# Two heads of attention on one core: TensorE in groups of two slots, 32-column tiles for all sums, denominators inverted through transposes, the subtraction shared out anew

## The chip, the cores and the metric

The kernel runs on one NeuronCore of a Trainium2 chip. The metric is the time of one execution on the device in microseconds (us), the median of the runs of a kernel. Engines are named as in the profile: PE is TensorE (matmuls; PEld its weight loads), DVE is VectorE, ACT is ScalarE, POOL is GpSimd, SP is SyncE, which issues most DMAs.

## The reference, cut to what matters

Two layers of self-attention over 2304 positions (48 x 48), with 2 images, 512 channels, 8 heads of 64. Layer 0 has a group norm in front; layer 1 adds a position embedding to what q and k are made of. All is float32.

```
# layer 0: x is (2, 512, 48, 48)
xn  = group_norm(x)
qkv = qkv_w @ xn + qkv_b            # per head: q, k, v of (64, 2304)
w   = softmax((q.T @ k) * 64**-0.5) # (2304, 2304) for each of 16 heads
x   = proj_w @ (v @ w.T) + proj_b + x
# layer 1: the same with other weights; q and k from [x, embedding], then
x   = softmax(q.T @ k / 8) @ v @ Wout + bout + x
```

## The kernel before, in words

Five stages follow one another: norm, q/k/v projection, attention of layer 0, projection out and q/k/v of layer 1, attention of layer 1, projection out. The change touches the attention stage alone (`attention_stage`), which runs twice.

A block is 384 queries of one pair of heads (e = 0, 1). There are 48 blocks in a stage, 96 in all. The 2304 keys are 18 tiles (kt) of 128, in 6 chunks (c) of 3. A block has 12 slots, s = 2c + e: one chunk of keys with one head. The work of a block is spread over some 30 slots, and each engine runs, slot by slot, a fixed list written out in its own `body`. At slot s of block t:

- TensorE (lines 735 to 748) waits until the banks of scores are free (`bank_free`: the copy of slot s - 2 is done, since slots use two sets of three PSUM banks in turn), makes the scores of slot s (L700: six matmuls of 128x128 by 384 columns), and then the sums of the slot 18 earlier (`weigh`): probabilities by v (L713, "PV", in 64-column tiles, one per head, bank 6) and probabilities by ones (L721, the denominators, in 32-column tiles, bank 7). Each float32 matmul of the sums is two records in the profile. `PV_TILES` and `DEN_PAIRS` say how many tiles of keys each slot takes: 1 or 2 (3 once, none once) and 0 to 2 pairs.
- VectorE takes the running maximum over keys (L851, from slot 2 of a block), at slots 10 and 11 also folds three running maxima into one (L856, L858), and subtracts the maximum from its part of the columns of the slot 15 earlier (`shift`, helper at L618: query columns 0 to 128 of 384, of three tiles).
- GpSimd subtracts the other columns (also L618: 128 to 384). It waits for the copy of the scores and, for the first two slots of a block, for the maximum; it runs as far ahead as these let it.
- ScalarE takes the exponential of the slot 16 earlier (L769), in place, which waits for both subtractions of it, and then copies the scores of slot s from PSUM into `prob` (L756) after VectorE's maximum has read them (from slot 2).

The maximum over the partitions goes through TensorE: `turn` at slots 0 and 1 (L677, transposes of the folded maxima), `reduce` on VectorE (L837), `broadcast_max` at slots 2 and 3 (L683, transposes), `copy_max` on ScalarE (L763). Slots 4 and 5 of TensorE also wait for that copy. The denominators: ScalarE copies the sums out (L781), TensorE spreads them by a matmul with a matrix of ones and zeros (L689, slot 8), ScalarE copies (L787), VectorE inverts in six parts of 64 columns (L871), and `norm` multiplies (L878). Waits on semaphores carry all of this order; SP loads q, k and v by the progress of `scored` and `pv_done`.

Of the kernel before, what the change touches and what calls it, by code (L numbers as in the profile page):

```python
# [7 lines left out]
ALU = mybir.AluOpType  # L8
# [3 lines left out]
P = 128  # L12
# [18 lines left out]
SHIFT_DVE = 128  # L31
# [3 lines left out]
PV_TILES = [[0, 1], [2], [3, 4], [5], [6, 7], [8], [9, 10], [11], [12, 13], [14], [15, 16, 17], []]  # L35
DEN_PAIRS = [[], [0], [], [1, 2], [], [3], [], [4, 5], [], [6], [], [7, 8]]
PV_END = 10
FREE_AT = [3, 3, 7, 7, 11, 11]
REDUCE_AT, BROADCAST_AT, SPREAD_AT = 0, 2, 8
INVERT_AT = [9, 12, 12, 13, 13, 14]  # L40
PARTS = len(INVERT_AT)
NORM_AT, STORE_AT = 3, 4
# [495 lines left out]
def attention_stage(nc, name, psum, bufs, qk_d, v_d, att_d, next_loads):  # L538
# [4 lines left out]

    with ExitStack() as ctx:  # L544
# [5 lines left out]
        den, dsp, pvr, rec, ob = bufs["den"], bufs["dsp"], bufs["pvr"], bufs["rec"], bufs["ob"]  # L550
        ones, sel, ident = bufs["ones"], bufs["sel"], bufs["ident"]
# [25 lines left out]
        def pv_count(t, v):  # L577
            return 2 * SLOTS + SLOTS * t + v + 1
# [51 lines left out]
        def _(sp):  # L630
            with sp.Fori(0, B) as b, sp.Fori(0, PAIRS) as hp:
                pair = b * PAIRS + hp
                for j in range(JB):
# [28 lines left out]
        def _(pe):  # L662
            pe.sem_inc(scored, 2 * SLOTS)
            pe.sem_inc(pv_done, 2 * SLOTS)

            def bank_free(t, s):
# [4 lines left out]
                if not before(t, 2) and s == SPREAD_AT + 2 and live(t - 2):  # L671
                    pe.wait_ge(spread_copied, t - 1)
# [32 lines left out]
            def weigh(t, par, v):  # L705
                if v == 0 and not before(t, 1):
                    pe.wait_ge(pv_copied, t)
                for kt in PV_TILES[v]:
                    if kt % 3 == 0:
                        pe.wait_ge(v_in[kt // 3], 16 * (t // JB + 1))  # L710
                        pe.wait_ge(exp_done, SLOTS * t + 2 * (kt // 3) + 2)
# [14 lines left out]
            def body(t, par):  # L726
                for s in range(SLOTS):
                    bank_free(t, s)
                    if not before(t, 1) and live(t - 1):
                        if s in (REDUCE_AT, REDUCE_AT + 1):  # L730
                            turn(t - 1, s, s - REDUCE_AT)
                        if s in (BROADCAST_AT, BROADCAST_AT + 1):
                            broadcast_max(t - 1, s, s - BROADCAST_AT)
                    if not before(t, 2) and live(t - 2) and s == SPREAD_AT:
                        spread_den(t - 2, s)
                    if live(t):
                        scores(t, par, s)
                    tv, pv, v = behind(t, par, s, PV_LAG)
                    if live(tv):
                        weigh(tv, pv, v)  # L740
# [4 lines left out]
        def _(act):  # L745
# [25 lines left out]
            def copy_weighted(t, par):  # L771
                act.wait_ge(pv_done, pv_count(t, PV_END))
                if not before(t, 2):
                    act.wait_ge(normed, t - 1)
                nc.scalar.activation(pvr[par][:, :], pv_bank, ACT.Copy).then_inc(pv_copied, 1)

            def copy_den(t):
                act.wait_ge(pv_done, pv_count(t, SLOTS - 1))
                if not before(t, 1):
                    act.wait_ge(spread, t)  # L780
                nc.scalar.activation(den[:, :], den_bank, ACT.Copy).then_inc(den_copied, 1)  # L781

            def copy_spread(t, s):
                act.wait_ge(spread, t + 1)
                if not before(t, 1):
                    act.wait_ge(inverted, PARTS * t)
                nc.scalar.activation(three(dsp[:, :]), spare(s), ACT.Copy).then_inc(spread_copied, 1)  # L787
# [8 lines left out]
            def body(t, par):  # L796
                for s in range(SLOTS):
                    te, pe_, se = behind(t, par, s, EXP_LAG)
                    if live(te):
                        exponential(te, pe_, se)  # L800
                    if s == 5 and not before(t, 2) and live(t - 2):
                        copy_weighted(t - 2, par)
                    if s == 6 and not before(t, 2) and live(t - 2):
                        copy_den(t - 2)
# [4 lines left out]
                    if s == SPREAD_AT and not before(t, 2) and live(t - 2):  # L809
                        copy_spread(t - 2, s)  # L810
# [8 lines left out]
        def _(pool):  # L819
            with pool.Fori(0, NB // 2) as it:  # L820
                for par in range(2):
                    t = 2 * it + par
                    for s in range(SLOTS):
                        if s < 2:
                            pool.wait_ge(mx_ready, unit(t, s))
                        pool.wait_ge(copied, SLOTS * t + s + 1)
                        shift_part(nc.gpsimd, par, s, SHIFT_DVE, CH).then_inc(pool_shifted, 1)

        @block.vector
        def _(dve):  # L830
# [35 lines left out]
            def invert(t, part):  # L866
                dve.wait_ge(spread_copied, t + 1)
# [5 lines left out]
            def norm(t, par):  # L873
                dve.wait_ge(inverted, PARTS * (t + 1))
# [3 lines left out]
                nc.vector.tensor_tensor(ob[par][:, :], pvr[par][:, :], rec[:, :], ALU.mult).then_inc(normed, 1)  # L878

            def body(t, par):  # L880
                for s in range(SLOTS):
                    if s in (REDUCE_AT, REDUCE_AT + 1) and not before(t, 1) and live(t - 1):
                        reduce(t - 1, s, s - REDUCE_AT)
# [5 lines left out]
                    for part in range(PARTS):  # L889
                        if INVERT_AT[part] == s and not before(t, 2) and live(t - 2):  # L890
                            invert(t - 2, part)
                        if INVERT_AT[part] == s + SLOTS and not before(t, 3) and live(t - 3):
                            invert(t - 3, part)
                    if s == NORM_AT and not before(t, 3) and live(t - 3):
                        norm(t - 3, 1 - par)
# [4 lines left out]
def program(nc, x, params, qkv_w, qkv_bv, proj_w, w1, w1v, w1e, wout, emb, consts, out):  # L900
# [9 lines left out]
    with ExitStack() as ctx:  # L910
        const_sb = sb_(ctx, nc, "const_sb", [P, 32 + 3 * P])
        par_sb = sb_(ctx, nc, "par_sb", [P, 2 * CT + 2 * CT + CT + CT])
        ones, sel, gmat = const_sb[:, 0:32], const_sb[:, 32:32 + P], const_sb[:, 32 + P:32 + 2 * P]
        ident = const_sb[:, 32 + 2 * P:32 + 3 * P]
# [157 lines left out]
```

## Time and profile before

| | |
|---|---|
| median of 3 runs | 4704.73 us (4703.88 to 4705.93) |
| the profiled execution | 4705.96 us, span of its instructions 4703.8 us |
| busy share of the span | PE 97%, PEld 52%, DVE 71%, ACT 60%, POOL 49% |
| granted TensorE clock, mean | 0.993 |
| attention stages | from about 410 to 2225 us and 2750 to 4570 us |

The profile is read in this order: the busy shares, the groups by line (how often, how long, what the idle time before them waited for), and then the timeline of each engine in one block. Ends of matmuls are modelled, so the distance from one start to the next says more about TensorE than the durations. "<-" names what ended an idle time.

### The profile page before, as it was taken

To read this page: it belongs to the slowest core of one execution; us is meant where nothing else is said; L and a number is where in the kernel's file an instruction comes from. 1 tells how busy PE (TensorE), PEld (TensorE's weight loads), DVE (VectorE), ACT (ScalarE), POOL (GpSimd) and SP (SyncE) were. 2 spreads that over 40 slices of the span, in tenths; PEclk is the share of its full clock that TensorE was granted. 3 is DMA by queue.
4 is the path that set the end of the run, shared out by engine and by line. 5 is a ranking of instruction groups with operands and counts; after the bars stand their busy time and mean duration, and the time that the engine had idled before them with its cause. 6 is when DMAs were issued, how large, how long until landed. Compare 5 with 4: busy or idle time off the path is not lost. (4 is left out here: it accounts for less than half of the span.)

```text
span 4703.8 us, 77022 instructions
## 1 busy us (share of the span) xinstructions
PE 4551.0 (97%) x25368; PEld 2453.8 (52%) x25368; DVE 3318.6 (71%) x3948; ACT 2820.0 (60%) x2981; POOL 2314.1 (49%) x1160
## 2 busy tenths in 40 slices
PE   7997999999999999998999979999999999999989
PEld 4554555555555555554555545555555555555545
DVE  4224888888888888888433358888888888888872
ACT  1113777777777777776001137777777777777750
POOL 0001666666666666666100026666666666666650
PEclk9999999999999999999999999999999999999999
DMA  4334121211111111110444431111111111111206
GB/s 192 131 124 118 25 61 28 54 35 45 42 45 45 37 45 35 48 43 32 167 146 149 147 104 31 50 38 42 46 41 45 37 47 34 50 37 45 59 20 214
DMA packets 234728, 321.66 MB, mean 68 GB/s; under 512 B 12080, under 2 KB 221104, under 8 KB 233648
## 3 DMA queue, kind: packets, MB, share of 16 engines
q1 hardware_dynamic: 214512, 292.61, 21.3%
q10 hardware_dynamic: 20160, 28.32, 1.6%
q8 instruction: 34, 0.56, 0.0%
q14 instruction: 22, 0.18, 0.0%
HBM read 188.76 MB, written 132.12 MB: 68 GB/s over the span
## 5 line engine op out<-in xcount | busy, mean ns | idle before, releaser
L618 POOL TENSOR_TENSOR prob<-prob,mx 128x768 f32<-128x768 f32 x1152 | 2293.1, 2025 | 2227.6 <-ACT mx L763 2227.6
L756 ACT ACTIVATE prob<-psum_att 128x1152 f32<-128x1152 f32 x1152 | 1302.3, 1130 | 587.1 <-DVE run L851 510.5
L700 PE MATMUL psum_att<-qst,kst 128*128 128x384 f32 x6912 | 1513.4, 354 | 44.6 <-DMA kst<-qk_scratch 27.4
L769 ACT ACTIVATE prob<-prob 128x1152 f32<-128x1152 f32 x1152 | 1340.8, 1164 | 356.2 <-DVE prob L618 355.2
L700 PEld LDWEIGHTS psum_att<-qst,kst 128*128 128x128 f32 x6912 | 1156.5, 189 | 452.3 <-issue 427.1
L713 PE MATMUL psum_att<-prob,vst 128*64 128x384 f32 x6912 | 1348.3, 502 | 15.4 <-ACT prob L769 9.2
L851 DVE TENSOR_TENSOR run<-psum_att,run 128x1152 f32<-128x1152 f32 x768 | 1039.1, 1353 | 370.1 <-PE psum_att L700 359.8
L618 DVE TENSOR_TENSOR prob<-prob,mx 128x384 f32<-128x384 f32 x1152 | 1015.5, 882 | 1.7 <-ACT mx L763 1.7
L713 PEld LDWEIGHTS psum_att<-prob,vst 128*64 128x64 f32 x6912 | 405.4, 136 | 532.1 <-issue 491.0
L721 PE MATMUL psum_att<-prob,const_sb 128*32 128x384 f32 x6912 | 677.1, 494 | 0.0
L321 PE MATMUL psum<-xc_l,wq 128*128 128x384 f32 x1536 | 504.1, 489 | 10.8 <-DVE hl_l L426 5.6
L851 DVE TENSOR_TENSOR run<-psum_att,prob 128x1152 f32<-128x1152 f32 x192 | 260.5, 1357 | 269.4 <-PE psum_att L700 269.3
L321 PEld LDWEIGHTS psum<-xc_l,wq 128*128 128x128 f32 x1536 | 293.8, 191 | 221.7 <-issue 20.3
L721 PEld LDWEIGHTS psum_att<-prob,const_sb 128*32 128x32 f32 x6912 | 165.6, 108 | 424.9 <-issue 423.7
L364 ACT ACTIVATE hl_l<-qk_sum 128x384 fp32r<-128x384 f32 x96 | 50.1, 522 | 444.9 <-DVE qk_sum L423 444.9
L871 DVE RECIPROCAL rec<-dsp 128x64 f32<-128x64 f32 x576 | 287.0, 526 | 12.1 <-ACT dsp L787 12.1
L186 PE MATMUL psum<-attc_l,wo_l 128*128 128x384 f32 x768 | 252.6, 490 | 6.3 <-PEq L544 6.3
L858 DVE TENSOR_TENSOR fold<-fold,run 128x384 f32<-128x384 f32 x192 | 248.7, 1295 | 6.6
L367 ACT ACTIVATE hl_l<-psum,par_sb 128x384 fp32r<-128x384 f32 x96 | 55.8, 581 | 309.2 <-PE psum L321 309.2
L186 PEld LDWEIGHTS psum<-attc_l,wo_l 128*128 128x128 f32 x768 | 147.2, 192 | 109.1 <-issue 8.9
L430 DVE SCALAR_TENSOR_TENSOR hl_l<-psum,par_sb,hl_l 128x384 fp32r<-128x384 f32 x96 | 59.3, 618 | 188.6 <-ACT hl_l L367 188.6
L677 PEld LDWEIGHTS psum_att<-const_sb,fold 128*128 128x128 f32 x576 | 59.9, 141 | 161.7 <-DVE fold L858 139.6
(53 smaller groups left out, 1633.6 us busy)
## 6 DMA issues: line engine op xcount, KB each, us to landing
qk_scratch<-hl_l SPq DMA_DIRECT2D x48, 1536.0 KB, 5.6
qst<-qk_scratch SPq DMA_DIRECT2D x192, 384.0 KB, 5.4
kst<-qk_scratch SPq DMA_DIRECT2D x192, 192.0 KB, 3.3
v_scratch<-vo_l SPq DMA_DIRECT2D x24, 768.0 KB, 3.5
vst<-v_scratch SPq DMA_DIRECT2D x96, 192.0 KB, 2.5
att_scratch<-ob ACTq DMA_DIRECT2D x96, 192.0 KB, 1.9
attc_l<-att_scratch SPq DMA_DIRECT2D x24, 768.0 KB, 6.0
x_sb<-in_x SPq DMA_DIRECT2D x8, 1152.0 KB, 14.3
```

Source lines behind the costliest of these rows:

```text
L186: mm = nc.tensor.matmul(bank, w[c], att[:, c, :], start=(c == 0), stop=(c == CT - 1))
L321: mm = nc.tensor.matmul(qk_bank(m), qkv["w"][:, c, m * P:(m + 1) * P], xc[p][:, c, :], start=(c == 0), stop=(c == CT - 1))
L618: return engine.tensor_tensor(x[:, :, q0:q1], x[:, :, q0:q1], m, ALU.subtract)
L677: mm = nc.tensor.transpose(spare_bank(s, r), fold[e][:, r * P:(r + 1) * P], ident)
L700: mm = nc.tensor.matmul(psum[:, 3 * (s % 2) + k, 0:CH], kst[:, e, (3 * c + k) * P:(3 * c + k + 1) * P], qst[par][:, 2 * w + e, :], start=( ...
L713: mm = nc.tensor.matmul(psum[e * D:(e + 1) * D, 6, 0:CH], vst[:, kt, e * D:(e + 1) * D], prob[par][:, e, kt, :], start=(kt == 0), stop=(kt ...
L721: mm = nc.tensor.matmul(psum[r:r + 32, 7, 0:CH], ones[:, :], prob[par][:, e, 2 * j + odd, :], start=(j == 0), stop=(j == KT // 2 - 1), til ...
L756: nc.scalar.activation(chunk_of(par, s), s_bank(s), ACT.Copy).then_inc(copied, 1)
L769: nc.scalar.activation(x, x, ACT.Exp, scale=SCALE).then_inc(exp_done, 1)
L851: nc.vector.tensor_tensor(r[:, :, :], s_bank(s), other, ALU.max).then_inc(maxed, 1)
L858: nc.vector.tensor_tensor(fold[e][:, :], fold[e][:, :], r[:, 2, :], ALU.max).then_inc(folded, 1)
L871: nc.vector.reciprocal(rec[:, q], dsp[:, q]).then_inc(inverted, 1)
```

## The change

- TensorE: a group is two slots. It makes the scores of slots 2c and 2c + 1, and then all sums of one chunk: three tiles of PV, then one or two pairs of denominators (`DEN_PAIRS` is now by chunk: 1, 2, 1, 2, 1, 2).
- PV is done in four 32-column tiles instead of two of 64 columns, with the same moving data for both halves of a head: twice the instructions.
- The denominators, copied out of PSUM, are transposed (slot 8), added in pairs and inverted as 128x6 numbers on VectorE, widened again to 128x384, transposed back (slot 10), and `norm` multiplies from PSUM. ScalarE's copy `dsp` is gone, and so are six reciprocals of 64 columns and the matmuls with `sel`.
- The copies of both sums (`copy_weighted`) stand at the head of ScalarE's slot 6.
- VectorE subtracts 208 of the 384 query columns instead of 128, GpSimd 176 instead of 256, and GpSimd waits for VectorE's subtraction of the same slot.

```diff
-SHIFT_DVE = 128
+SHIFT_DVE = 208
+POOL_BEHIND = True
 SHIFT_LAG = 15
 EXP_LAG = 16
 PV_LAG = 18
-PV_TILES = [[0, 1], [2], [3, 4], [5], [6, 7], [8], [9, 10], [11], [12, 13], [14], [15, 16, 17], []]
-DEN_PAIRS = [[], [0], [], [1, 2], [], [3], [], [4, 5], [], [6], [], [7, 8]]
+PV_COLS = 32
+DEN_PAIRS = [[0], [1, 2], [3], [4, 5], [6], [7, 8]]
+TURN_AT, BROADCAST_AT = 0, 2
+EVACUATE_AT, DEN_TURN_AT, DEN_SPREAD_AT = 6, 8, 10
+STORE_AT = 0
...
-            def spread_den(t, s):
+            def turn_den(t, s):
                 pe.wait_ge(den_copied, t + 1)
                 for r in range(3):
-                    mm = nc.tensor.matmul(spare_bank(s, r), sel, den[:, r * P:(r + 1) * P], start=True, stop=True)
+                    mm = nc.tensor.transpose(spare_bank(s, r), den[:, r * P:(r + 1) * P], ident)
+                mm.then_inc(den_turned, 1)
+
+            def spread_den(t, s):
+                pe.wait_ge(widened, t + 1)
+                for r in range(3):
+                    mm = nc.tensor.transpose(spare_bank(s, r), dwide[:, r, :], ident)
                 mm.then_inc(spread, 1)
...
-            def weigh(t, par, v):
-                if v == 0 and not before(t, 1):
+            def weigh(t, par, c):
+                if c == 0 and not before(t, 1):
                     pe.wait_ge(pv_copied, t)
...
+                pe.wait_ge(v_in[c], 16 * (t // JB + 1))
+                pe.wait_ge(exp_done, SLOTS * t + 2 * c + 2)
+                for kt in range(3 * c, 3 * c + 3):
                     for e in range(2):
-                        mm = nc.tensor.matmul(psum[e * D:(e + 1) * D, 6, 0:CH], vst[:, kt, e * D:(e + 1) * D],
-                                              prob[par][:, e, kt, :], start=(kt == 0), stop=(kt == KT - 1))
-                for j in DEN_PAIRS[v]:
+                        for d in range(e * D, (e + 1) * D, PV_COLS):
+                            mm = nc.tensor.matmul(psum[d:d + PV_COLS, 6, 0:CH], vst[:, kt, d:d + PV_COLS],
+                                                  prob[par][:, e, kt, :], start=(kt == 0), stop=(kt == KT - 1),
+                                                  tile_position=(0, d))
+                for j in DEN_PAIRS[c]:
...
             def body(t, par):
-                for s in range(SLOTS):
-                    bank_free(t, s)
...
+                for c in range(KC):
+                    for s in (2 * c, 2 * c + 1):
+                        bank_free(t, s)
+                        if not before(t, 1) and live(t - 1):
+                            if s in (TURN_AT, TURN_AT + 1):
+                                turn(t - 1, s, s - TURN_AT)
+                            if s in (BROADCAST_AT, BROADCAST_AT + 1):
+                                broadcast_max(t - 1, s, s - BROADCAST_AT)
+                        if not before(t, 2) and live(t - 2):
+                            if s == DEN_TURN_AT:
+                                turn_den(t - 2, s)
+                            if s == DEN_SPREAD_AT:
+                                spread_den(t - 2, s)
+                        if live(t):
+                            scores(t, par, s)
+                    tv, pv, sv = behind(t, par, 2 * c, PV_LAG)
                     if live(tv):
-                        weigh(tv, pv, v)
+                        weigh(tv, pv, sv // 2)
...
@@ GpSimd @@
                         pool.wait_ge(copied, SLOTS * t + s + 1)
+                        if POOL_BEHIND:
+                            pool.wait_ge(dve_shifted, SLOTS * t + s + 1)
                         shift_part(nc.gpsimd, par, s, SHIFT_DVE, CH).then_inc(pool_shifted, 1)
...
@@ VectorE @@
+            def invert(t, s):
+                dve.wait_ge(den_turned, t + 1)
+                if live(t + 2):
+                    dve.wait_ge(scored, scored_count(SLOTS * (t + 2) + s))
                 if not before(t, 1):
-                    dve.wait_ge(normed, t)
-                q = slice(part * CH // PARTS, (part + 1) * CH // PARTS)
-                nc.vector.reciprocal(rec[:, q], dsp[:, q]).then_inc(inverted, 1)
+                    dve.wait_ge(inverted, t)
+                groups = spare(s).rearrange("p r (e o i) -> p r e o i", e=2, o=2)[:, :, :, :, 0]
+                nc.vector.tensor_reduce(dsum[:, :, :], groups, AX.X, ALU.add).then_inc(den_summed, 1)
+                dve.wait_ge(den_summed, t + 1)
...
+                nc.vector.reciprocal(dcol[:, :, :], dsum[:, :, :]).then_inc(inverted, 1)
+                dve.wait_ge(inverted, t + 1)
...
+                nc.vector.tensor_copy(dwide.rearrange("p r (e i) -> p r e i", e=2),
+                                      dcol[:, :, :].unsqueeze(3).broadcast_to([P, 3, 2, D])).then_inc(widened, 1)
+
+            def norm(t, par, s):
+                dve.wait_ge(spread, t + 1)
+                if live(t + 2):
+                    dve.wait_ge(scored, scored_count(SLOTS * (t + 2) + s))
                 dve.wait_ge(pv_copied, t + 1)
...
-                nc.vector.tensor_tensor(ob[par][:, :], pvr[par][:, :], rec[:, :], ALU.mult).then_inc(normed, 1)
+                nc.vector.tensor_tensor(three(ob[par][:, :]), spare(s), three(pvr[:, :]), ALU.mult).then_inc(normed, 1)

             def body(t, par):
                 for s in range(SLOTS):
-                    if s in (REDUCE_AT, REDUCE_AT + 1) and not before(t, 1) and live(t - 1):
-                        reduce(t - 1, s, s - REDUCE_AT)
+                    if s in (TURN_AT, TURN_AT + 1) and not before(t, 1) and live(t - 1):
+                        reduce(t - 1, s, s - TURN_AT)
+                    if not before(t, 2) and live(t - 2):
+                        if s == DEN_TURN_AT:
+                            invert(t - 2, s)
+                        if s == DEN_SPREAD_AT:
+                            norm(t - 2, par, s)
                     if live(t) and s >= 2:
                         maximum(t, par, s)
                     ts, ps, ss = behind(t, par, s, SHIFT_LAG)
                     if live(ts):
                         shift(ts, ps, ss)
```

## Rows read from the trace of the kernel before

**Rows 1.** The page's first part: busy us (share) x instructions of each engine.
```profile
PE 4551.0 (97%) x25368; PEld 2453.8 (52%) x25368; DVE 3318.6 (71%) x3948; ACT 2820.0 (60%) x2981; POOL 2314.1 (49%) x1160
```

**Rows 2.** Groups by line and form: busy us, mean ns, idle before and its releasers.
```profile
L618 POOL TENSOR_TENSOR prob<-prob,mx 128x768 f32<-128x768 f32 x1152 | 2293.1, 2025 | 2227.6 <-ACT mx L763 2227.6
L618 DVE TENSOR_TENSOR prob<-prob,mx 128x384 f32<-128x384 f32 x1152 | 1015.5, 882 | 1.7 <-ACT mx L763 1.7
```

**Rows 3.** One line's instructions: one L775 per block, 38 between 3000 and 4400 us.
```profile
L775 ACT ACTIVATE pvr<-psum_att x38: 468/472/474, 3016.9 to 4392.5; 128x384 f32<-128x384 f32 x38
```

**Rows 4.** Timeline of TensorE's matmuls: start us, us to the modelled end, instruction.
```profile
2873.14 0.87 PE L713 MATMUL psum_att<-prob,vst 128*64 128x384 f32 x4
2873.94 0.85 PE L721 MATMUL psum_att<-prob,const_sb 128*32 128x384 f32 x8
2874.72 0.94 PE L689 MATMUL psum_att<-den,const_sb 128*128 128x128 f32 x6
2875.41 1.29 PE L700 MATMUL psum_att<-qst,kst 128*128 128x384 f32 x6
2876.64 1.51 PE L713 MATMUL psum_att<-prob,vst 128*64 128x384 f32 x8
2878.08 1.31 PE L700 MATMUL psum_att<-qst,kst 128*128 128x384 f32 x6
```

**Rows 5.** The same timeline where transposes stand ahead of the scores.
```profile
2860.09 0.54 PE L683 MATMUL psum_att<-const_sb,mcol 128*128 128x128 f32 x3
2860.38 1.29 PE L700 MATMUL psum_att<-qst,kst 128*128 128x384 f32 x6
```

**Rows 6.** Timeline of VectorE: maxima and what follows them; between the last two rows two folds.
```profile
2861.71 1.36 DVE L851 TENSOR_TENSOR run<-psum_att,prob 128x1152 f32<-128x1152 f32 x1 [0.67 <-PE psum_att L700]
...
2879.43 1.36 DVE L851 TENSOR_TENSOR run<-psum_att,run 128x1152 f32<-128x1152 f32 x1 [0.35 <-PE psum_att L700]
2880.71 0.55 DVE L618 TENSOR_TENSOR prob<-prob,mx 128x384 f32<-128x384 f32 x1
2881.17 0.55 DVE L871 RECIPROCAL rec<-dsp 128x64 f32<-128x64 f32 x1
...
2887.65 1.34 DVE L851 TENSOR_TENSOR run<-psum_att,run 128x1152 f32<-128x1152 f32 x1
...
2890.10 0.55 DVE L618 TENSOR_TENSOR prob<-prob,mx 128x384 f32<-128x384 f32 x1
```

**Rows 7.** Timeline of ScalarE: exponential, copy, exponential; the copy of the maximum.
```profile
2853.52 1.17 ACT L769 ACTIVATE prob<-prob 128x1152 f32<-128x1152 f32 x1 [0.52 <-DVE prob L618]
2854.60 1.11 ACT L756 ACTIVATE prob<-psum_att 128x1152 f32<-128x1152 f32 x1
2855.61 1.15 ACT L769 ACTIVATE prob<-prob 128x1152 f32<-128x1152 f32 x1
...
2861.17 0.48 ACT L763 ACTIVATE mx<-psum_att 128x384 f32<-128x384 f32 x1
```

**Rows 8.** GpSimd: one in the timeline; two by line (min/median/max ns).
```profile
2861.82 1.84 POOL L618 TENSOR_TENSOR prob<-prob,mx 128x768 f32<-128x768 f32 x1 [12.14 <-ACT mx L763]
...
L618 POOL TENSOR_TENSOR prob<-prob,mx x2: 1837/2008/2178, 2864.8 to 2866.6; 128x768 f32<-128x768 f32 x2
```

**Rows 9.** The first slots of layer 0, where ScalarE waits for GpSimd, TensorE for ScalarE.
```profile
L618 POOL TENSOR_TENSOR prob<-prob,mx x1: 1831/1831/1831, 451.3 to 451.3; 128x768 f32<-128x768 f32 x1
...
453.20 1.28 ACT L769 ACT_TABLE_LOAD   x1 [0.24 <-POOL prob L618]
455.57 1.11 ACT L756 ACTIVATE prob<-psum_att 128x1152 f32<-128x1152 f32 x1
456.73 1.65 PE L700 MATMUL psum_att<-qst,kst 128*128 128x384 f32 x4 [1.55 <-ACT prob L756]
```

**Rows 10.** Groups by line and form: a small reciprocal, and GpSimd's other operation.
```profile
L130 DVE RECIPROCAL gn_rstd<-gn_sd 128x4 f32<-128x4 f32 x2 | 0.4, 178 | 0.5 <-ACT gn_sd L104 0.5
L240 POOL TENSOR_TENSOR emb_table<-emb_parts 128x2304 f32<-128x2304 f32 x4 | 20.8, 5225 | 17.9 <-ACT emb_parts L350 17.9
```

More of the change, by code:

```diff
@@ L670, in bank_free @@
                     pe.wait_ge(mx_ready, unit(t - 1, s - BROADCAST_AT - 2))
-                if not before(t, 2) and s == SPREAD_AT + 2 and live(t - 2):
-                    pe.wait_ge(spread_copied, t - 1)
+                if not before(t, 2) and s == DEN_TURN_AT + 2 and live(t - 2):
+                    pe.wait_ge(den_summed, t - 1)
+                if not before(t, 3) and s == DEN_SPREAD_AT + 2 - SLOTS and live(t - 3):
+                    pe.wait_ge(normed, t - 2)
             def turn(t, s, e):
@@ L769, in exponential, with copy_weighted @@
                 nc.scalar.activation(x, x, ACT.Exp, scale=SCALE).then_inc(exp_done, 1)
[L771 to L778, printed above, removed]
+            def copy_weighted(t):
+                act.wait_ge(pv_done, pv_count(t, KC - 1))
                 if not before(t, 1):
-                    act.wait_ge(spread, t)
+                    act.wait_ge(normed, t)
+                    act.wait_ge(den_turned, t)
+                nc.scalar.activation(pvr[:, :], pv_bank, ACT.Copy).then_inc(pv_copied, 1)
                 nc.scalar.activation(den[:, :], den_bank, ACT.Copy).then_inc(den_copied, 1)
[L783 to L787, printed above, removed]
             def store(t, par):
@@ L797, in body @@
                 for s in range(SLOTS):
+                    if s == EVACUATE_AT and not before(t, 2) and live(t - 2):
+                        copy_weighted(t - 2)
                     te, pe_, se = behind(t, par, s, EXP_LAG)
@@ L800, in body @@
                         exponential(te, pe_, se)
[L801 to L804, printed above, removed]
                     if live(t):
@@ L808, in body @@
                         copy_max(t - 1, 1 - par, s, s - BROADCAST_AT)
-                    if s == SPREAD_AT and not before(t, 2) and live(t - 2):
-                        copy_spread(t - 2, s)
                     if s == STORE_AT and not before(t, 3) and live(t - 3):
@@ L864, in shift @@
                 shift_part(nc.vector, par, s, 0, SHIFT_DVE).then_inc(dve_shifted, 1)
-            def invert(t, part):
-                dve.wait_ge(spread_copied, t + 1)
+            def invert(t, s):
+                dve.wait_ge(den_turned, t + 1)
+                if live(t + 2):
+                    dve.wait_ge(scored, scored_count(SLOTS * (t + 2) + s))
                 if not before(t, 1):
-                    dve.wait_ge(normed, t)
-                q = slice(part * CH // PARTS, (part + 1) * CH // PARTS)
-                nc.vector.reciprocal(rec[:, q], dsp[:, q]).then_inc(inverted, 1)
-            def norm(t, par):
-                dve.wait_ge(inverted, PARTS * (t + 1))
+                    dve.wait_ge(inverted, t)
+                groups = spare(s).rearrange("p r (e o i) -> p r e o i", e=2, o=2)[:, :, :, :, 0]
+                nc.vector.tensor_reduce(dsum[:, :, :], groups, AX.X, ALU.add).then_inc(den_summed, 1)
+                dve.wait_ge(den_summed, t + 1)
+                if not before(t, 1):
+                    dve.wait_ge(widened, t)
+                nc.vector.reciprocal(dcol[:, :, :], dsum[:, :, :]).then_inc(inverted, 1)
+                dve.wait_ge(inverted, t + 1)
+                if not before(t, 1):
+                    dve.wait_ge(spread, t)
+                nc.vector.tensor_copy(dwide.rearrange("p r (e i) -> p r e i", e=2),
[4 more added lines that the diff above has]
+                    dve.wait_ge(scored, scored_count(SLOTS * (t + 2) + s))
                 dve.wait_ge(pv_copied, t + 1)
@@ L888, in body @@
                         shift(ts, ps, ss)
[L889 to L895, printed above, removed]
             blocks(dve, body)
```

58 lines of the change are left out of this document (17 added, 41 removed).

## The prediction, made before the changed kernel ran

> **What bounds the kernel now.** I read the busy shares first: TensorE is busy 97% of the span [rows 1]. Since ends of matmuls are modelled, I then took the block's length and added up TensorE's start-to-start distances. One L775 stands in each block: 38 of them lie 1375.6 us apart, so a block takes 1375.6 / 37 = 37.18 us [rows 3], and 96 blocks 3569 us of 4704.
>
> From the timeline [rows 4], per step:
> - scores to PV: 1.23 us (2875.41 to 2876.64); six score matmuls of 384 columns take six times some 0.16, so 0.97, and entering the tiles costs 0.27.
> - one tile of keys of PV (four records): 1.51 - 0.87 = 0.64, say 0.645. Eight records and out again to the scores: 2878.08 - 2876.64 = 1.44, so leaving costs 0.15.
> - PV to denominators: 0.80 (2873.14 to 2873.94), so 0.155 for going from 64 to 32 columns. One pair (eight records) and out: 0.78, so 0.63 to 0.645 per pair.
> - the spread of the denominators 0.69; three transposes 0.29 [rows 5].
>
> Before, a block is 12 x 0.97 + 18 x 0.645 + 9 x 0.645 + 12 x 0.27 + 12 x 0.15 + 5 x 0.155 + 4 x 0.29 + 0.69 = 36.7 us. So TensorE's own work sets the block, and 0.5 us are waits.
>
> The other engines have room, but VectorE and GpSimd get in each other's way: VectorE's subtraction takes 0.55 alone [rows 6] and 0.88 in the mean, GpSimd's 1.84 alone [rows 8] and 2.03 in the mean [rows 2]; one that met a subtraction of VectorE took 2.18 [rows 8]. This costs TensorE next to nothing now.
>
> **The change on TensorE.** PV in four 32-column tiles: eight records per tile of keys. The trace has no such PV, but the denominators are eight records in four 32-column tiles at 0.645, the same time in which two 64-column tiles do a tile of keys. So I cost the finer tiles at nothing (bounds: nothing, and 0.645 more per tile of keys if the two halves of a head did not run side by side). Group of two slots: entering and leaving happens 6 times instead of 12: -6 x 0.42 = -2.5. PV to denominators is no change of tile size any more: -5 x 0.155 = -0.8 (bounds 0 and 0.155 each; nearest is the run inside the 32-column tiles, 0). The spread is two times three transposes instead of 0.69: -0.1. Sum -3.4: TensorE alone would need 3 x (5.58 + 4.94) + 6 x 0.29 = 33.3 us per block.
>
> The Trainium skill, TensorEngine Tiling (Array Packing), Key Properties, says that changing the tiling mode drains TensorE while changing the tile inside a mode does not. For this change it says that the step from PV to denominators is free; were it not, each group would be 0.155 longer, 0.47 us per block on the path worked out below.
>
> **The change on the others.** VectorE's subtraction has 3 x 208 = 624 elements instead of 384. Its price alone: 0.55 for 384 and 1.36 for 1152 [rows 6] give 1.05 ns an element, so 0.80 (bounds 0.74 and 0.89, in proportion). GpSimd's has 528 instead of 768: 1.84 x 528/768 = 1.26 if there is no fixed part, 1.84 if nothing falls; with L240's 5.225 for 2304 elements [rows 10] the slope is 2.2 ns and the result 1.31, which I take. The six reciprocals (6 x 0.46) and two disturbed folds go from VectorE, ScalarE loses one copy; the new inversion is three small dependent operations at slot 8 (0.18 for a reciprocal [rows 10], some 0.9 in all, bounds 0.5 and 1.5). These are no bound: ScalarE's work per block is 12 x (1.08 + 1.01) [rows 7] and four small copies, 27 us, VectorE's 10 x 1.28 + 12 x (0.80 - 0.09) and some 5 for the rest, 26.5 (0.09 is what one overlaps with the next, 0.55 against 0.46 [rows 6]).
>
> The Trainium skill, GPSIMD Engine Reference, on the measured tensor_tensor of 2048 float32, gives 4497 ns. As an estimate, with this case's 1.84 for 768 it makes 1.34 for 528, and 0.1 us more per block than my 1.31.
>
> **What is late next.** The change adds a wait: GpSimd starts its part only after VectorE's. Behind GpSimd's part stands the exponential, and behind the exponential, in ScalarE's queue, the copy that frees the score banks. So follow one group k, scores of its first slot (2k) starting at a(k), of the second at b(k):
> 1. scores to maximum 1.35 (2878.08 to 2879.43) [rows 4, 6];
> 2. maximum to VectorE's subtraction of the slot 15 earlier 1.28 [rows 6];
> 3. that subtraction 0.80;
> 4. GpSimd's start after a release: 0.17, as 2861.17 + 0.48 to 2861.82 [rows 7, 8] (bounds 0.05 and 0.17);
> 5. GpSimd 1.31;
> 6. to ScalarE 0.08 (451.29 + 1.83 to 453.20) [rows 9];
> 7. exponential to copy, starts, 1.08 [rows 7]: it is the copy of slot 2k+1, since the exponential at slot s is of the slot subtracted at s - 1;
> 8. the copy 1.11 and 0.05 to TensorE [rows 9].
>
> That copy frees the bank for slot 2k+3, the second slot of the next group: b(k+1) is at least a(k) + 7.2. And a(k+2) = b(k+1) + 0.97 + 0.27 + 1.94 + (0.645 or 1.29) + 0.15 = b(k+1) + 3.97 or 4.62, by one or two pairs. Without waits b(k+1) would be at a(k) + 5.9 or 6.5: TensorE waits, with the sums queued behind the scores it cannot start. In the kernel before the same two places lay three single slots apart (about 9.3 us), and the chain was 1.35 + 1.28 + 0.88 + 1.08 + 1.16 = 5.8.
>
> Going round a block by odd k (slots 2, 6, 10), where the groups between (k = 2, 4, 0) have two pairs:
> - k=1: 6.1 to the copy's start; slot 5 also waits for the copy of the maximum behind it: 1.01 + 0.48 + 0.05 [rows 7]. With the group: 7.6 + 4.6 = 12.2.
> - k=3: 7.2 + 4.6 + 0.3 (transposes at slot 10) = 12.1.
> - k=5: norm ahead of the maximum (0.46, as between short operations in [rows 6]), two folds between maximum and subtraction (2890.10 - 2887.65 = 2.45 instead of 1.28), transposes at slots 1 and 2: 7.2 + 0.46 + 1.17 + 0.3 + 4.6 + 0.3 = 14.1.
>
> Sum 38.4 us. By even k it is 34.5 (the inversion lies there), so it doesn't decide. A block of 38.4 against 37.18: +1.2 x 96 = +117 us. Of the profiled execution's 4705.96 (1.2 over the median, 2.2 over its span) this makes 4823, against the median 4822. Where GpSimd then runs, it will run beside VectorE's maximum, which reads PSUM; the 1.84 at 2861.82 [rows 8] was beside one, 2861.71 [rows 6], so I add no contention. First and last blocks, projections, loads: unchanged, cost nothing.
>
> Ends of the terms, each three times per block, by 96: GpSimd 1.26 to 1.84 is -14 to +153 us; its start -35; VectorE's part -17 to +26; PV to denominators +45. Taken together not all at one end: the likeliest case's own range is 4770 to 4900.
>
> **Rivals.**
> - TensorE stays the bound, the chain is hidden. For it: TensorE is at 97%, and ScalarE and VectorE have over 4 us per block to spare. Against it: each link is a wait in the code, with its time in a row. 33.3 + 0.5 of waits as now: 33.8, so -3.4 x 96 = -326, 4380.
> - The chain holds but is shorter, since spans on GpSimd are rough: at 0.65 us less a round, 38.4 - 1.95 = 36.4, -70 us, 4635. It decides from 0.4 us less per round on (3 x 0.4 = 1.2).
> - GpSimd's part hardly falls with its columns (1.6) and the step PV to denominators keeps its 0.155: 38.4 + 0.87 + 0.47 = 39.7, +245 us, 4950.
> - The finer PV tiles don't run side by side: 33.3 + 18 x 0.645 = 44.9 us per block, +740, 5450. The denominators of the same shape speak against it; 1 in 100.
>
> **Numbers.** Forecast 0.58; TensorE-bound 0.10; shorter chain 0.16; a block within 0.1 us of today's 0.06; 4950 or above 0.10. A measurement here tells 0.2% (9 us) from no change. Faster 0.26, same 0.06, slower 0.68. The range 4620 to 4920 leaves out the TensorE-bound case and the tails of the others.
>
> **What would show it.** In the profile after: waits of L700 on the copy L756 in the hundreds of us in total, at odd slots, largest (2 to 3 us) at slot 1 and about 1 us at slots 5 and 9; waits of the exponential on POOL instead of DVE; DVE's subtraction at 0.80 and POOL's at 1.31 with almost no spread; PV's eight records 0.645 apart and no gap to the denominators; no wait at a first slot of a group. I am wrong if L700 shows hardly any wait (then a block is near 33.3), or if GpSimd ends well before ScalarE asks for it.

## The result, and the profile after

The changed kernel takes 4981.17 us (median of 4 runs, 4975.42 to 4982.91) against 4705.33 before: ratio 1.0584, 95% interval 1.0565 to 1.0602. Slower was forecast (4822, range 4620 to 4920), but the time lies outside the range: +276 us instead of +117.

The profiled execution took 4975.42 us. The first part of its page, and the groups that answer to [rows 1, 2]; columns as there:

```profile
PE 4452.7 (90%) x32280; PEld 2549.7 (51%) x32280; DVE 3027.2 (61%) x3660; ACT 2784.3 (56%) x2885; POOL 1552.7 (31%) x1160
```

```profile
L618 POOL TENSOR_TENSOR prob<-prob,mx 128x528 f32<-128x528 f32 x1152 | 1531.7, 1330 | 3262.3 <-DVE prob L618 3258.7
L618 DVE TENSOR_TENSOR prob<-prob,mx 128x624 f32<-128x624 f32 x1152 | 1091.7, 949 | 6.9 <-ACT mx L776 6.9
```

TensorE's matmuls and the three other engines are busy for less time than before; only the weight loads, which overlap the matmuls, take more (2549.7 against 2453.8 us). So the added time is waiting, or the clock. Who waits for whom (us in total, times, longest):

```profile
ACT prob L782 <- POOL prob L618: 681.6, 603, 2.4
PEld psum_att L708 <- ACT prob L769: 262.0, 214, 3.1
PE psum_att L679 <- ACT prob L769: 234.1, 94, 3.9
PE psum_att L708 <- ACT mx L776: 110.7, 94, 1.2
```

ScalarE's exponential (now L782) waits for GpSimd, and TensorE for ScalarE's copies (L769, and L776 of the maximum): once in each block at each of three places. L679 is the transpose at slot 1, which comes behind the wait for the bank; L708 is the scores.

The blocks, cut from one L789 (the copy of the PV sum) to the next: length, busy time of PE, PEld, DVE, ACT, POOL, granted clock, DMA share, GB/s. The first five of a row of 13:

```profile
3011.98:3050.77 38.79, 34.65 (x307) 20.19 (x308) 28.17 (x32) 27.84 (x29) 15.79 (x13) 1.00 0.10 26
3050.77:3091.26 40.49, 36.11 (x307) 20.88 (x308) 27.59 (x32) 27.84 (x29) 15.86 (x13) 0.96 0.21 53
3091.26:3131.81 40.55, 36.14 (x307) 20.57 (x308) 27.80 (x32) 27.80 (x29) 15.86 (x13) 0.96 0.21 55
3131.81:3172.40 40.59, 36.20 (x307) 20.60 (x308) 28.21 (x32) 27.80 (x30) 15.88 (x13) 0.96 0.10 29
3172.40:3211.34 38.94, 34.53 (x307) 20.20 (x308) 28.17 (x32) 27.82 (x29) 15.87 (x13) 1.00 0.22 50
```

The pattern repeats, sometimes with four slow blocks in a row: one block of 38.8 to 39.1 us at full clock, then three of 40.4 to 40.7 in which the clock was lower for a while. Over both stages 94 stretches lie between two such copies of one stage, and 71 of them hold a drop of the clock. So there are two terms: 38.9 against 37.18 is +1.7 us a block, 165 us in all; and 1.6 us more in three blocks of four, 0.75 x 1.6 x 96 = 115. Together 280, of 276 measured.

TensorE in the first of these blocks (start us, us to the modelled end, instruction [idle before]). The scores (L708) of slots 6 and 7 start at 3011.85, of 8 at 3017.18, of 9 at 3019.10, of 10 and 11 at 3024.01, of 0 at 3029.43, of 1 at 3033.32, of 2 at 3038.20, of 5 at 3046.06; L721 is PV, L730 the denominators:

```profile
3011.85 2.38 PE L708 MATMUL psum_att<-qst,kst 128*128 128x384 f32 x12
3014.16 2.14 PE L721 MATMUL psum_att<-prob,vst 128*32 128x384 f32 x24
3016.12 0.83 PE L730 MATMUL psum_att<-prob,const_sb 128*32 128x384 f32 x8
3016.88 0.55 PE L691 MATMUL psum_att<-const_sb,den 128*128 128x128 f32 x3
3017.18 1.30 PE L708 MATMUL psum_att<-qst,kst 128*128 128x384 f32 x6
3019.10 1.32 PE L708 MATMUL psum_att<-qst,kst 128*128 128x384 f32 x6 [0.62 <-ACT prob L769]
...
3024.01 2.46 PE L708 MATMUL psum_att<-qst,kst 128*128 128x384 f32 x12
3026.41 2.14 PE L721 MATMUL psum_att<-prob,vst 128*32 128x384 f32 x24
3028.36 0.83 PE L730 MATMUL psum_att<-prob,const_sb 128*32 128x384 f32 x8
3029.12 0.55 PE L679 MATMUL psum_att<-const_sb,fold 128*128 128x128 f32 x3
3029.43 1.30 PE L708 MATMUL psum_att<-qst,kst 128*128 128x384 f32 x6
3033.02 0.54 PE L679 MATMUL psum_att<-const_sb,fold 128*128 128x128 f32 x3 [2.30 <-ACT prob L769]
3033.32 1.29 PE L708 MATMUL psum_att<-qst,kst 128*128 128x384 f32 x6
...
3038.20 1.29 PE L708 MATMUL psum_att<-qst,kst 128*128 128x384 f32 x6
...
3046.06 1.28 PE L708 MATMUL psum_att<-qst,kst 128*128 128x384 f32 x6 [1.22 <-ACT mx L776]
...
3050.63 1.68 PE L708 MATMUL psum_att<-qst,kst 128*128 128x384 f32 x8
```

The waits stand where they were forecast: before the second scores of a group, at slots 9 (0.62 us), 1 (2.30 here, 2.5 in the blocks behind it) and 5 (1.22). Between the first scores of slot 10 (3024.01) and those of slot 1 the path can be followed link by link. VectorE, GpSimd and ScalarE, each from its own timeline; the last rows of VectorE and ScalarE belong to slot 2's maximum and to the wait at slot 5:

```profile
3025.88 1.35 DVE L852 TENSOR_TENSOR run<-psum_att,run 128x1152 f32<-128x1152 f32 x1
...
3028.33 0.80 DVE L618 TENSOR_TENSOR prob<-prob,mx 128x624 f32<-128x624 f32 x1
...
3039.71 1.36 DVE L852 TENSOR_TENSOR run<-psum_att,prob 128x1152 f32<-128x1152 f32 x1 [3.13 <-PE psum_att L708]
```

```profile
3029.27 1.33 POOL L618 TENSOR_TENSOR prob<-prob,mx 128x528 f32<-128x528 f32 x1 [4.32 <-DVE prob L618]
```

```profile
3030.70 1.16 ACT L782 ACTIVATE prob<-prob 128x1152 f32<-128x1152 f32 x1 [2.31 <-POOL prob L618]
3031.76 1.11 ACT L769 ACTIVATE prob<-psum_att 128x1152 f32<-128x1152 f32 x1
...
3045.43 0.48 ACT L776 ACTIVATE mx<-psum_att 128x384 f32<-128x384 f32 x1
```

VectorE's part ends at 3029.13, GpSimd starts 0.14 later, ScalarE's exponential 0.10 after GpSimd's end, the copy ends at 3032.87, TensorE goes on at 3033.02, 0.15 later.

Where the clock fell, stretches of the third block (columns as for the blocks above):

```profile
3109.60:3112.40 2.80, 0.37 (x3) 0.05 (x1) 2.73 (x6) 2.18 (x2) 0.93 (x2) 1.00 1.02 240
3112.40:3114.20 1.80, 1.74 (x9) 1.44 (x9) 1.50 (x1) 0.87 (x1) 0.99 (x2) 0.81 0.25 44
3114.20:3117.50 3.30, 3.30 (x25) 1.03 (x28) 1.48 (x2) 3.30 (x4) 2.46 (x2) 0.59 0.17 60
3117.50:3122.00 4.50, 4.50 (x42) 3.12 (x38) 1.25 (x1) 1.23 (x2) 0.00 (x0) 1.00 0.00 0
```

TensorE had done almost nothing for 2.8 us (the wait at slot 1), and then worked partly at the lower of its two levels (1.2 GHz): 0.81 and 0.59 are means of stretches that hold both, and the 2 us from 3114.40 on have 0.50. PV and denominators there:

```profile
3114.34 3.39 PE L721 MATMUL psum_att<-prob,vst 128*32 128x384 f32 x24
3117.56 1.46 PE L730 MATMUL psum_att<-prob,const_sb 128*32 128x384 f32 x16
```

PV took 3.22 us from its start to the denominators' instead of 1.96. The fifth block above had the same wait at slot 1 (2.50 us) and no drop, so the wait's length alone does not say which block is hit.

### The profile page after: what moved, and what is told of

The parts are those of the page before. It is cut to its first block and busy times, and to the rows that moved or that the text cites. A ratio compares the mean times of both kernels' runs of the same rounds, so it can differ in the third digit from the quotient of the medians.

```text
span 4973.6 us, 91164 instructions
## 1 busy us (share of the span) xinstructions
PE 4452.7 (90%) x32280; PEld 2549.7 (51%) x32280; DVE 3027.2 (61%) x3660; ACT 2784.3 (56%) x2885; POOL 1552.7 (31%) x1160
## 5 line engine op out<-in xcount | busy, mean ns | idle before, releaser
L618 POOL TENSOR_TENSOR prob<-prob,mx 128x528 f32<-128x528 f32 x1152 | 1531.7, 1330 | 3262.3 <-DVE prob L618 3258.7
L782 ACT ACTIVATE prob<-prob 128x1152 f32<-128x1152 f32 x1152 | 1343.4, 1166 | 683.1 <-POOL prob L618 681.6
L708 PE MATMUL psum_att<-qst,kst 128*128 128x384 f32 x6912 | 1500.1, 357 | 224.3 <-ACT mx L776 110.7
L769 ACT ACTIVATE prob<-psum_att 128x1152 f32<-128x1152 f32 x1152 | 1291.3, 1121 | 570.4 <-DVE run L852 513.7
L708 PEld LDWEIGHTS psum_att<-qst,kst 128*128 128x128 f32 x6912 | 1195.9, 193 | 409.8 <-ACT prob L769 262.0
L721 PE MATMUL psum_att<-prob,vst 128*32 128x384 f32 x13824 | 1309.9, 515 | 8.2 <-ACT prob L782 8.2
L618 DVE TENSOR_TENSOR prob<-prob,mx 128x624 f32<-128x624 f32 x1152 | 1091.7, 949 | 6.9 <-ACT mx L776 6.9
L721 PEld LDWEIGHTS psum_att<-prob,vst 128*32 128x32 f32 x13824 | 407.3, 114 | 666.8 <-issue 601.8
L730 PE MATMUL psum_att<-prob,const_sb 128*32 128x384 f32 x6912 | 662.6, 486 | 0.0
L730 PEld LDWEIGHTS psum_att<-prob,const_sb 128*32 128x32 f32 x6912 | 223.4, 110 | 338.3 <-issue 338.3
L679 PE MATMUL psum_att<-const_sb,fold 128*128 128x128 f32 x576 | 107.7, 298 | 238.7 <-ACT prob L769 234.1
L679 PEld LDWEIGHTS psum_att<-const_sb,fold 128*128 128x128 f32 x576 | 60.5, 142 | 327.7 <-issue 250.0
L892 DVE TENSOR_TENSOR ob<-psum_att,pvr 128x384 f32<-128x384 f32 x96 | 53.6, 558 | 203.6 <-PE psum_att L708 190.9
```

Source lines behind the costliest of these rows:

```text
L618: return engine.tensor_tensor(x[:, :, q0:q1], x[:, :, q0:q1], m, ALU.subtract)
L679: mm = nc.tensor.transpose(spare_bank(s, r), fold[e][:, r * P:(r + 1) * P], ident)
L708: mm = nc.tensor.matmul(psum[:, 3 * (s % 2) + k, 0:CH], kst[:, e, (3 * c + k) * P:(3 * c + k + 1) * P], qst[par][:, 2 * w + e, :], start=( ...
L721: mm = nc.tensor.matmul(psum[d:d + PV_COLS, 6, 0:CH], vst[:, kt, d:d + PV_COLS], prob[par][:, e, kt, :], start=(kt == 0), stop=(kt == KT - 1),
L730: mm = nc.tensor.matmul(psum[r:r + 32, 7, 0:CH], ones[:, :], prob[par][:, e, 2 * j + odd, :], start=(j == 0), stop=(j == KT // 2 - 1), til ...
L769: nc.scalar.activation(chunk_of(par, s), s_bank(s), ACT.Copy).then_inc(copied, 1)
```

## The experiments

Two theories stood after the result. Theory 1: the path that the prediction followed sets the block, and the drop of the clock is what the longest wait on it brings with it (1a; 1b is that the 1.6 us come from something else). Theory 2: the two-slot groups or the 32-column tiles cost TensorE the time by themselves. All edits are to the changed kernel unless it says otherwise.

**The exponential one slot later.**
```diff
-EXP_LAG = 16
+EXP_LAG = 17
```


> EXP_LAG 17 instead of 16, nothing else: the exponential of a slot comes two slots after VectorE's subtraction, not one, so GpSimd's part has a whole slot more before ScalarE asks for it. Theory 1 (the path scores, maximum, VectorE's part, GpSimd's part, exponential, copy, second scores of the next group sets the block; the dropped clock is its follower): ScalarE no longer waits for GpSimd, the block falls from 40.1 us to about 35.5 (33.3 of TensorE, 1.3 left at slot 1 where the folds stand ahead of the second maximum, 0.8 at slot 5 behind the copy of the maximum), granted clock back to 0.99: 4545 us, between 4400 and 4650. Theory 2 (the two-slot group or the 32-column tiles themselves cost TensorE the time): within 50 us of the changed kernel's 4981.

Measured: 4569.68 us, ratio to before 0.9706 (0.969 to 0.9722), mean clock 0.993, inside the range. One constant takes 411 us away. Its blocks are like this one:

```profile
3014.79:3050.59 35.80, 34.24 (x307) 20.26 (x308) 28.55 (x32) 27.39 (x28) 15.99 (x13) 1.00 0.11 27
```

Theory 2 falls: groups, tiles, transposes and the sharing of the subtraction are all in it. It is also the fastest version here, faster than both kernels. Its longest wait in a block is now for the fold, at slot 1:

```profile
3069.49 0.54 PE L679 MATMUL psum_att<-const_sb,fold 128*128 128x128 f32 x3 [1.19 <-DVE fold L859]
```

**GpSimd free again.**
```diff
-POOL_BEHIND = True
+POOL_BEHIND = False
```


> POOL_BEHIND False: GpSimd again runs ahead, with 176 columns, VectorE with 208. Theory 1: two links (0.15 and 1.33 us) leave the path at each of the three deciding places, VectorE's and GpSimd's parts get in each other's way again (VectorE's 0.95 goes to 1.1 to 1.2, folds up to 2 us longer): block about 36 us, 4600 us, between 4500 and 4700; ScalarE's waits are for VectorE. Theory 2: within 50 us of 4981, or slower by the contention.

Measured: 4616.27 us, ratio 0.9808 (0.9791 to 0.9824), inside the range; blocks of 36.3 to 36.4 us, clock 1.00. The wait that the change added is the one that costs: 365 us hang on it, after what its absence costs (VectorE's part takes 1.21 us in the mean instead of 0.95).

**Work for TensorE in its longest wait.** A block of zeros is put behind the constants (those lines are left out here), and multiplied into the open sums.
```diff
                     for s in (2 * c, 2 * c + 1):
+                        if s == 1 and not before(t, 2) and live(t - 2):
+                            for _ in range(8):
+                                nc.tensor.matmul(psum[:, 6, 0:P], bufs["zeros"], ident, start=False, stop=False)
                         bank_free(t, s)
```


> The changed kernel with eight float32 matmuls of a 128x128 zero matrix by 128 columns (sixteen records, some 1.8 us) added into the open sums at slot 1, ahead of TensorE's longest wait (2.3 to 2.5 us); they add zero. Theory 1a (three blocks in four lose 1.6 us to a granted clock of 0.5 that follows this wait): no drop of the clock in the steady blocks, all take 38.9 us: 4981 - 115 = 4866 us, between 4840 and 4890. Theory 1b (the clock's drop costs nothing that the waits would not cost anyway, the 1.6 us come from something else): 4981 within 20, or more by up to 96 x 1.8 if the fillers are not hidden by the wait.

Measured: 4867.93 us, ratio 1.0343 (1.0325 to 1.036). Two of its blocks; they and the seven behind them take 38.93 to 38.99 us at clock 1.00:

```profile
3032.89:3071.86 38.97, 36.34 (x323) 22.15 (x324) 28.14 (x32) 27.85 (x30) 15.87 (x13) 1.00 0.21 57
3071.86:3110.79 38.93, 36.33 (x323) 22.15 (x324) 28.23 (x32) 27.80 (x30) 15.88 (x13) 1.00 0.10 30
```

More work on TensorE made the kernel 113 us faster, as theory 1a had it (115). The blocks are as long as the changed kernel's at full clock, so the path is as it was; only TensorE's idle time at slot 1 fell from 2.5 to 0.7 us. What is left over the forecast, 4868 against 4822, is the path itself.

**PV in 64-column tiles.**
```diff
-PV_COLS = 32
+PV_COLS = 64
```


> PV back in two 64-column tiles (PV_COLS 64), all else as changed. Theory 1: a tile of keys costs the same 0.645 us either way, but going from PV to the denominators costs 0.155 us in each group again, three times on the deciding path: +0.47 us per block, +45 us, 5026 (5010 to 5050). Theory 2 (32-column tiles cost TensorE time): faster than 4981 by more than 20 us.

Measured: 5043.34 us, ratio 1.0716 (1.0698 to 1.0734): 62 us slower than the changed kernel, inside the range. A block at full clock and two of those that follow it:

```profile
3041.77:3080.95 39.18, 35.51 (x235) 20.11 (x236) 28.09 (x32) 27.83 (x29) 15.74 (x13) 1.00 0.10 26
3080.95:3121.78 40.83, 36.91 (x235) 21.30 (x236) 27.54 (x32) 27.83 (x29) 15.83 (x13) 0.96 0.21 54
3121.78:3162.70 40.92, 36.95 (x235) 21.28 (x236) 27.54 (x32) 27.88 (x29) 15.83 (x13) 0.96 0.20 54
```

Blocks with the drop are 40.9 instead of 40.55 (+0.4, of 0.47 expected): from PV to the denominators is now 2.08 us (3083.10 to 3085.18) instead of 1.96. And nearly all blocks have the drop, 89 of 94 instead of 71, 18 x 1.6 = 29 us. The wait at slot 1 was shorter, 2.35 us, than the changed kernel's 2.5. So the finer tiles are worth 30 to 40 us on the path, and cost nothing; the rest of the 62 is the clock, which the expectation had left out.

**VectorE takes 256 columns, GpSimd 128.**
```diff
-SHIFT_DVE = 208
+SHIFT_DVE = 256
```


> The changed kernel with VectorE 256 of 384 columns, GpSimd 128. Theory 1: on the path VectorE's link grows by 144 elements (0.80 to 0.95 us), GpSimd's shrinks by 144 (1.33 to 1.03 at 2.1 ns an element): 0.15 less at each of three places, 0.45 per block, -43 us: 4938 (4920 to 4955), more only if fewer blocks lose time to the clock. Theory 2 (VectorE's load decides): slower than 4981.

Measured: 4892.5 us, ratio 1.0395 (1.0379 to 1.0411): 89 us faster than the changed kernel, outside the 4920 to 4955. Two consecutive blocks of it:

```profile
3003.97:3044.05 40.08, 36.18 (x307) 20.58 (x308) 29.13 (x32) 27.68 (x29) 12.09 (x13) 0.96 0.22 55
3044.05:3082.54 38.49, 34.55 (x307) 20.25 (x308) 29.12 (x32) 27.71 (x29) 12.11 (x13) 1.00 0.22 57
```

The path shrank by 0.45 us a block as worked out (38.94 to 38.49). The rest is what the expectation named as a condition and put at nothing: every second block (48 of 94) loses 1.6 us, not three in four, 0.25 x 1.6 x 96 = 38 us. 43 + 38 = 81 of the 89. The wait at slot 1 was 2.34 us in blocks with and without the drop, as long as with 64-column PV, where nearly every block was hit.

**The new sharing alone, in the kernel before.**
```diff
-SHIFT_DVE = 128
+SHIFT_DVE = 208
...
                         pool.wait_ge(copied, SLOTS * t + s + 1)
+                        pool.wait_ge(dve_shifted, SLOTS * t + s + 1)
```


> The kernel before with the new sharing of the subtraction alone: VectorE 208 columns, GpSimd 176, GpSimd behind VectorE. Theory 1: GpSimd's link lengthens the path to 7.2 us (8.4 at slot 10, where the folds stand), but in single slots the copy is asked for only some 9.3 us after the scores, so the new wait costs nothing, and folds and subtractions are no longer disturbed: the 0.5 us of waits per block shrink, 4680 us (4655 to 4705). Theory 2 (GpSimd behind VectorE is slow by itself, whatever the groups): slower than before by over 1%.

Measured: 4698.95 us, ratio 0.9982 (0.9973 to 0.9991). It is inside the range. GpSimd behind VectorE costs next to nothing where TensorE works slot by slot, although ScalarE waits for it just as much:

```profile
ACT prob L769 <- POOL prob L618: 727.9, 891, 2.3
```

The gain is 8 us, less than the 27 expected: TensorE's wait for the fold fell from 38.6 to 4.5 us in total, but its wait before PV for the exponential, which now stands behind GpSimd, rose from 9.2 to 35.8.

**Both: exponential later and GpSimd free.**
```diff
-EXP_LAG = 16
+EXP_LAG = 17
...
-POOL_BEHIND = True
+POOL_BEHIND = False
```


> The changed kernel with both: exponential one slot later (EXP_LAG 17) and GpSimd free. Theory 1: GpSimd is off the deciding path either way once the exponential is later, so all that is left of the second edit is the contention with the folds and VectorE's parts, which stand ahead of the second maximum at slots 10 and 11: 4570 plus 0 to 2 us per block, 4650 (4570 to 4760). Rival (a free GpSimd is worth something by itself): below 4560.

Measured: 4621.35 us, ratio 0.9817 (0.9802 to 0.9832), inside the range, 52 us slower than with the later exponential alone. Its groups at L618:

```profile
L618 POOL TENSOR_TENSOR prob<-prob,mx 128x528 f32<-128x528 f32 x1152 | 1778.3, 1578 | 2655.0 <-ACT mx L776 2655.0
L618 DVE TENSOR_TENSOR prob<-prob,mx 128x624 f32<-128x624 f32 x1152 | 1390.4, 1208 | 8.3 <-ACT mx L776 8.3
```

VectorE's part takes 1.21 us in the mean instead of the 1.02 of the later exponential alone, GpSimd's 1.58 instead of 1.34. TensorE waits 1.34 us at slot 11, where VectorE's drawn-out parts delay the maximum and the copy, in place of 1.19 for the fold at slot 1, and a block takes 36.4 us instead of 35.8. So putting GpSimd behind VectorE is worth 52 us, once nothing on the path waits for it.

**VectorE's part of slot 10 behind the folds of slot 11** (with the exponential one slot later).
```diff
-                    ts, ps, ss = behind(t, par, s, SHIFT_LAG)
-                    if live(ts):
-                        shift(ts, ps, ss)
+                    for sh in () if s == SLOTS - 2 else (s - 1, s) if s == SLOTS - 1 else (s,):
+                        ts, ps, ss = behind(t, par, sh, SHIFT_LAG)
+                        if live(ts):
+                            shift(ts, ps, ss)
```


> Exponential one slot later, and VectorE's part of the subtraction of slot 10 moved behind the maximum and folds of slot 11. With the later exponential alone a block is 35.8 us, with 1.5 us of wait at slot 1 for the fold and 0.7 at slot 5. The move takes 0.72 us off the path to that fold: 35.1 us per block, 4503 us (4490 to 4530). If the wait at slot 1 is for ScalarE's copy as much as for the fold, the gain is smaller but not nothing, since the copy of slot 11 waits for the same maximum.

Measured: 4737.28 us, ratio 1.0063 (1.0049 to 1.0077): 168 us slower than without the move, where 67 faster was expected. A miss. TensorE at slots 0 and 1 of one block, and ScalarE there:

```profile
3093.41 0.54 PE L679 MATMUL psum_att<-const_sb,fold 128*128 128x128 f32 x3 [0.47 <-DVE fold L859]
3093.71 1.29 PE L708 MATMUL psum_att<-qst,kst 128*128 128x384 f32 x6
3097.20 2.14 PE L721 MATMUL psum_att<-prob,vst 128*32 128x384 f32 x24 [2.20 <-ACT prob L782]
```

```profile
3095.98 1.16 ACT L782 ACTIVATE prob<-prob 128x1152 f32<-128x1152 f32 x1 [2.71 <-POOL prob L618]
```

The wait for the fold did fall (1.19 to 0.47 us). But the two parts moved together came late, GpSimd's behind them, and the exponential in ScalarE's slot 0 behind that. PV of the same group needs it: a new wait of 2.2 us for the 0.7 that was won. The block grew from 35.8 to 37.35 us, 148 us in all, and in 13 of 94 blocks the clock dropped, some 20 us.

**VectorE 160 columns, GpSimd 224** (with the exponential one slot later).
```diff
-SHIFT_DVE = 208
+SHIFT_DVE = 160
```


> Exponential one slot later (EXP_LAG 17) and VectorE 160 of 384 columns, GpSimd 224. GpSimd is off the deciding path, so its longer part (1.6 us) costs nothing; VectorE's part falls from 0.80 to 0.65 and stands once between the maximum of slot 10 and the fold for which TensorE waits 1.2 us at slot 1, and once at slot 5: 0.15 to 0.3 us per block less, 4555 us (4540 to 4570). Rival: GpSimd's longer part meets VectorE's again (1.6 us do not fit beside a maximum of 1.28) and the gain is lost: 4570 or more.

Measured: 4586.52 us, ratio 0.9744 (0.9731 to 0.9757), 17 us slower than with 208, where 15 faster was expected. The rival of the expectation came out: GpSimd's 1.64 us outlast a maximum of VectorE, and the next part or fold is disturbed (a fold of 0.89 instead of 0.56 us, at 3039.89).

**PV between the two scores of a group.**
```diff
                         if live(t):
                             scores(t, par, s)
-                    tv, pv, sv = behind(t, par, 2 * c, PV_LAG)
-                    if live(tv):
-                        weigh(tv, pv, sv // 2)
+                        tv, pv, sv = behind(t, par, 2 * c, PV_LAG)
+                        if live(tv):
+                            weigh(tv, pv, sv // 2, s % 2)
```
`weigh` is split (those lines are left out here): with 0 as its last argument it makes PV, with 1 the denominators.


> The changed kernel with TensorE's order inside a group changed alone: scores of the first slot, PV of the chunk, scores of the second slot, denominators. ScalarE, VectorE and GpSimd as changed, GpSimd behind VectorE. Theory 1 (the path binds because the second scores stand right behind the first and the sums behind their wait): the second scores are now asked for some 10 us after the first scores of the group before, not 6.5, the path of 7.2 to 8.9 us is hidden, and TensorE pays six more entries and exits of the tiles, 2.5 us per block: 35.8 us, plus up to 1 us where PV of a new block waits for the copy of the old sums: 4570 to 4670, clock back at 0.99. Theory 2 (GpSimd behind VectorE with a lag of one slot is what costs, whatever the order on TensorE): within 100 us of 4981.

Measured: 4752.06 us, ratio 1.0095 (1.008 to 1.0111), blocks of 37.7 us, clock 1.00. That is 229 us faster than the changed kernel, so the order on TensorE is a part of the cause, as theory 1 says; but it is 82 us above the range. Its TensorE has no wait left before second scores and two others instead:

```profile
3027.54 2.14 PE L723 MATMUL psum_att<-prob,vst 128*32 128x384 f32 x24 [0.93 <-ACT prob L786]
...
3046.54 2.14 PE L723 MATMUL psum_att<-prob,vst 128*32 128x384 f32 x24 [0.71 <-ACT pvr L793]
```

The second was expected. The first, 0.9 us a block or 88 us, is what the range left out. It is the same path, met one link earlier: PV itself waits for the exponential behind GpSimd.

## Why the prediction was wrong, by its own steps

**What holds.** TensorE's own work behind the waits: PV of three tiles in 32 columns to denominators 3016.12 - 3014.16 = 1.96 (1.94 forecast), no price for the step to the denominators; with 64 columns a price of 0.12 came back. VectorE's part 0.80 on the path and GpSimd's 1.33 (0.80 and 1.31 forecast). GpSimd's start 0.14, its release of ScalarE 0.10 (0.17 and 0.08). The three places of the waits and their order of size. The even groups did not decide. The later exponential hid the path, as a path through it must allow.

**What was off beside the path.** VectorE's part was forecast with almost no spread; 464 of its 1152 parts ran beside one of GpSimd's for a while and took 1.17 us in the mean (3032.71: 1.73), so the mean of all was 0.95. Two slots' scores to PV take 2.31 (3011.85 to 3014.16) instead of 2.21, 0.1 in each of six groups. Neither lay on the path.

**Where the sum was short on the path.** Forecast 38.4 us a block, measured 38.9, +48 us (46 by the filler's run). By the starts of the scores: slot 6 to slot 9 is 3019.10 - 3011.85 = 7.25 (7.2 forecast); slot 10 to slot 1 is 3033.32 - 3024.01 = 9.3 (9.1); slot 2 to slot 5 is 3046.06 - 3038.20 = 7.9 (7.6). About 0.1 of each of the last two is the way from ScalarE to TensorE, 0.15 (3045.43 + 0.48 to 3046.06 at slot 5) instead of the 0.05 taken from [rows 9]. Slot 2's maximum also started 1.51 us after the scores (3039.71) instead of 1.35; why, is open. These are mis-sized terms; alone they would have given some 4870, within the likeliest case's own range (4770 to 4900).

**The step that failed.** "A block of 38.4 against 37.18: +1.2 x 96 = +117 us". This priced each of TensorE's waits at its own length and kept the clock of the kernel before. Neither the sum nor an end of the range nor a rival had a term for a lower clock behind a wait. In the kernel before there was none to read: between 2800 and 4500 us TensorE waited at most 1.7 us, and its steady blocks had the clock at 1.00. But the path itself had worked out a wait of 2.7 us at slot 1 (9.15 less the 6.5 that TensorE needs). The runs showed what came with it: the clock was lower in three blocks of four, at 1.6 us each, 115 us. That the idle time is the cause is shown by the filler, which left the path as it was and took 113 us away. With this term the forecast would have been 4937; with the path's 48 us, 4985, against 4981.

**The rivals.** None came out. The one at 4950 is near the measured time, but by another mechanism (a longer GpSimd part and a kept step of 0.155); its terms were measured and are not there.

## What to carry to other kernels

Before two steps on the busiest engine are put together to save its overhead, count for each wait how far its releaser now stands ahead, in the new order: here 7.2 us of links fitted into three single slots (9.3 us) and not into a group and a half (5.9 to 6.5 us). An extra wait that is nearly free in one order (8 us gained with the new sharing) cost 365 us in the other, and one more slot of lag kept the gains of both, 4570 us. When a forecast leaves TensorE a wait of the length seen here (2.2 us and more), add a term for its clock: from nothing to what was lost here, 1.6 us for each such wait.

## What the runs showed of the hardware

- Behind waits at slot 1 of 2.5 us TensorE's clock was at the lower level for a while in 71 of 94 blocks, and a block then took 1.6 us longer. With longest waits of 1.2 us (blocks of 35.8 us) and 1.3 us (36.4 us) the granted clock stayed at 1.00. Eight small matmuls in the wait, which left 0.7 us of it idle, kept it at 1.00 too.
- The length of the wait does not say how many blocks are hit: 2.2 us hit 13 of 94 (blocks of 37.35 us at full clock), 2.34 us 48 of 94 (38.5 us), 2.35 us 89 of 94 (PV in 64 columns). What else decides is open.
- Four 32-column tiles of PV took the time of two of 64 columns (0.65 us per tile of keys), with twice the instructions. From 32-column PV to the denominators there was no step; from 64-column PV it was 0.12 us.
- VectorE's and GpSimd's parts of the in-place subtraction disturb each other when they overlap (means of 1.21 and 1.58 us with GpSimd free, against 0.80 and 1.33 undisturbed; single parts of VectorE took up to 1.96), while GpSimd beside VectorE's maximum, which reads PSUM, kept its 1.33. The Trainium skill, GPSIMD Engine Reference, Key points, says that GpSimd contends with VectorE instructions in a 2-port perf mode or with two SBUF inputs; for the second these runs agree, the subtraction of 1.21 against 0.80 us having two SBUF inputs.
